# Delta rule by chunks of 64 tokens in place of 128, in a kernel of two layers

## The reference

```python
def step(S, inp):                                   # once a token
    q_t, k_t, v_t, b_t = inp
    pred = jnp.einsum('bhk,bhkv->bhv', k_t, S)
    delta = (v_t - pred) * b_t[..., None]
    S = S + k_t[..., :, None] * delta[..., None, :]
    o_t = jnp.einsum('bhk,bhkv->bhv', q_t, S)
```

## Time and profile before

| | us |
|---|---|
| median of 3 runs | 1889.7 |
| lowest of them | 1884.84 |
| the profiled execution: its time | 1893.3 |
| its span | 1891.7 |

### The profile page before, as it was taken

The page is one execution under the profiler, slowest core; times in us unless marked ns, Lnnn a source line. Parts: engine busy times, 40 slices in busy tenths (PEclk is TensorE's granted clock), DMA queues, the critical chain, the costliest instruction groups (busy, mean ns, idle before and its releaser), DMA issues. The chain is left out here.

```text
span 1891.7 us, 44267 instructions
## 1 busy us (share of the span) xinstructions
PE 1692.1 (89%) x16808; PEld 1123.2 (59%) x16808; DVE 1315.8 (70%) x3530; ACT 959.6 (51%) x2513; POOL 827.6 (44%) x827
## 2 busy tenths in 40 slices
PE   2698789998999999999999989999898999999787
PEld 1474557565775657656684657656575566755443
DVE  2654577767677778677777778687777778676373
ACT  1434544476345854467445754457534664456324
POOL 1725654554326444365436535265334554264000
PEclk9889989999799999999999999999989999999888
DMA  5220122201311023101222023200221013210020
GB/s 214 68 58 12 35 62 72 63 11 33 88 58 51 11 67 97 52 21 33 52 77 71 8 47 92 77 18 22 65 82 52 19 36 89 75 29 10 14 78 7
DMA packets 162147, 100.56 MB, mean 53 GB/s; under 512 B 59256, under 2 KB 149496, under 8 KB 161656
## 3 DMA queue, kind: packets, MB, share of 16 engines
q1 hardware_dynamic: 161648, 96.92, 19.2%
q10 hardware_dynamic: 288, 0.81, 0.2%
HBM read 55.36 MB, written 27.26 MB: 44 GB/s over the span
## 5 line engine op out<-in xcount | busy, mean ns | idle before, releaser
L1360 ACT ACTIVATE shared<-bank 128x512 f32<-128x512 f32 (+1 forms) x384 | 201.8, 532 | 205.9 <-PE bank L1067 203.6
L1834 POOL TENSOR_TENSOR soft<-soft,prec 128x512 f32<-128x512 f32 x128 | 132.5, 1041 | 371.8 <-DVE prec L1478 371.4
L1642 DVE TENSOR_REDUCE nmx<-bank 128x1 f32<-128x512 f32 (+3 forms) x352 | 222.9, 637 | 93.3 <-PE bank L1039 91.6
L1260 ACT ACTIVATE soft<-bank,nmax 128x128 f32<-128x128 f32 x512 | 180.2, 380 | 105.7 <-DVE nmax L1470 104.7
L1795 POOL TENSOR_TENSOR qk_rs<-qk_rs,minus_half 128x16 f32<-128x16 f32 x64 | 187.7, 2934 | 5.3
L718 PE MATMUL bank<-w_sb,hT 128*128 128x512 f32 x256 | 137.3, 627 | 5.6 <-DVE rot L1460 3.1
L1067 PE MATMUL bank<-shared 75*128 75x384 bf16 (+3 forms) x512 | 140.4, 302 | 0.0
L1066 PE MATMUL bank<-b_sb 128*128 128x128 bf16 x512 | 113.8, 224 | 25.6 <-ACT shared L1360 22.8
L1039 PE MATMUL bank<-shared 72*128 72x256 bf16 (+3 forms) x512 | 126.8, 300 | 0.0
L688 PE MATMUL bank<-c_sb,soft 128*128 128x128 f32 x608 | 98.6, 294 | 24.1 <-POOL soft L1834 18.1
L1066 PEld LDWEIGHTS bank<-b_sb 128*128 128x128 bf16 x512 | 48.9, 98 | 115.8 <-ACT shared L1360 70.3
(11 more groups left out here) (254 smaller groups left out, 4492.6 us busy)
## 6 DMA issues: line engine op xcount, KB each, us to landing
shared<-parts_dram SPq DMA_DIRECT2D x64, 288.0 KB
vm<-v_f SPq DMA_DIRECT2D x112, 128.0 KB, 2.4
parts_dram<-parts SPq DMA_DIRECT2D x96, 128.0 KB, 2.4
L_dram<-the SPq DMA_DIRECT2D x32, 256.0 KB, 2.3
shared<-Z_dram SPq DMA_DIRECT2D x32, 256.0 KB, 3.5
shared<-L_dram SPq DMA_DIRECT2D x32, 256.0 KB, 4.4
shared<-X_dram SPq DMA_DIRECT2D x32, 256.0 KB, 4.9
w_sb<-weights SPq DMA_DIRECT2D x1, 4167.0 KB, 19.7
```

What stands on the lines that cost most here:

```text
L1260: a = af(v4(p_sb, 2, 4)[:, j, g], place("fS", j)[:, g * P:(g + 1) * P], ACT.Exp, bias=nmax[:, at:at + 1], accum_out=psums[:, at:at + 1])
L1360: af(v4(PTm, 2, GROUP)[:, u % 2, i, 0:n], place("mST", b, i)[:, 0:n], ACT.Exp).then_inc(mexp_done, 1)
L1642: reduce(v3(nmx[:], HM)[:, h:h + len(heads), c], v3(place("mS", b, t)[:, 0:len(heads) * (c + 1) * P], len(heads)), AX, ALU.max, negate=Tru ...
L1834: tt(p, p, spread(prec[:, at:at + NPAIR], P), ALU.mult).then_inc(fnorm_done, 1)
```

## The change

A chunk of 128 tokens keeps its projections, its gram matrix and its mask step, but the sequence goes over halves of 64 tokens (`r` = 0, 1; s = 2c + r counts 8 of them). The inverse then ends at blocks of 64, so `LEVELS` is 3 and level 3 is gone; level 2 is now the last, and forms no X and no zero fill. `seq_p` no longer projects V: `vb` does it once a batch for all four chunks and DVE scales it by beta, so that R becomes two DVE operations; the first half of a sequence has S = 0, no `seq_p`, and takes `vb` as its R. `U_sb` holds two tiles, each with 64 rows that stay zero, so K' U and O still contract over 128 rows. K' U now goes ahead of O on PE. The last inverse product's own waits go, `inv_v` of chunk 0 waits for `vb` besides. All five tables of `ORDER` are new; of them the diff shows two lines.

```diff
-LEVELS = 4
+LEVELS = 3
+SUB = 64
+NS = T // SUB
...
-     "fefefededffefdddefeeeeffebefefbbbbfffbffbbfbfbfddddbfddfddbbddbddddbddbdddedbdbddbdbdbddddbdbbddbbddddbbdbddddff"
+     "fefefefefefdefeeeeffebeeffbbbbfffffbdbddddfbbfbbfddddbffddddbdbdbddbdbddddddddbdbddbdddbdbddddebdbbbbbddbdbddddfd"
...
-        R_sb, U_sb, Sn = sb("R_sb", P), sb("U_sb", P), sb("Sn", H0 * DV)
+        R_sb, U_sb, Sn = sb("R_sb", P), sb("U_sb", 2 * P), sb("Sn", H0 * DV)
...
+                def vb_(b):
+                    pe.wait_ge(qT_copied, H0 * (b + 1))
+                    for c in range(NT):
+                        m = mm(place("vb")[:, c * P:(c + 1) * P], xnT[:, c * P:(c + 1) * P], W("wv"), start=True, stop=True)
+                    m.then_inc(bg_psum, 1)
...
                     for h in range(H0):
-                        m = mm(place("B", c)[:, h * P:(h + 1) * P], kc[:, h], qT[:, h * T + c * P:h * T + (c + 1) * P], start=True, stop=True)
+                        for r in range(2):
+                            at = h * T + c * P + SUB * r
+                            m = mm(place("B", c)[rows(r), h * SUB:(h + 1) * SUB], kc[:, h, rows(r)], qT[:, at:at + SUB], start=True, stop=True,
+                                   skip_group_check=True)
...
+                def seq_p(b, c, r):
+                    s = 2 * c + r
+                    if c and r == 0:
+                        pe.wait_ge(o_copied, NT * b + c)
+                    pe.wait_ge(S_done, (NS - 1) * b + s)
+                    for h in range(H0):
+                        at = slice(h * DV, (h + 1) * DV)
+                        m = mm(place("P", c)[rows(r), at], v4(kT, NT, H0)[:, c, h, rows(r)], Sn[:, at], start=True, stop=True,
+                               skip_group_check=True)
+                    m.then_inc(P_psum, 1)
+
+                def seq_u(b, c, r):
+                    s = 2 * c + r
+                    if s:
+                        pe.wait_ge(R_done, (NS - 1) * b + s)
+                    right = R_sb if s else vb
+                    for h in range(H0):
+                        m = mm(place("U", c)[rows(r), h * DV:(h + 1) * DV], v4(Z, NT, H0)[rows(r), c, h, rows(r)],
+                               right[rows(r), h * DV:(h + 1) * DV], start=True, stop=True, skip_group_check=True)
+                    m.then_inc(U_psum, 1)
...
+                    tt(v3(vb, NT * H0), v3(place("vb")[:], NT * H0), spread(beta[:], DV), ALU.mult).then_inc(gs_done, 1)
...
+                    link(tt(v3(R_sb[rows(r)], H0), v3(place("P", c)[rows(r), 0:P], H0), spread(beta[rows(r), c * H0:(c + 1) * H0], DV), ALU.mult))
+                    tt(R_sb[rows(r)], R_sb[rows(r)], cols(vb, c, P)[rows(r)], ALU.add).then_inc(R_done, 1)
```

More of the change, by code:

```diff
@@ L47 @@
[L47 to L56, removed]
@@ L139, in constants @@
     i, j = np.arange(P)[:, None], np.arange(P)[None, :]
-    c = {"ident": np.eye(P, dtype=f), "strict": (j < i).astype(f), "upper": -(i <= j).astype(f)}
-    low = [-((i >> (k + 1) == j >> (k + 1)) & ((i >> k) & 1 == 1) & ((j >> k) & 1 == 0)).astype(f) for k in range(4, 7)]
+    c = {"ident": np.eye(P, dtype=f), "strict": (j < i).astype(f), "upper": -(i % SUB <= j[:, :SUB]).astype(f)}
+    low = [-((i >> (k + 1) == j >> (k + 1)) & ((i >> k) & 1 == 1) & ((j >> k) & 1 == 0)).astype(f) for k in range(4, 3 + LEVELS)]
     half = np.arange(0, DF, 2, dtype=f)
@@ L214, in steps_delta @@
 def steps_delta(b):
-    s = [("qT", b, h) for h in range(H0)] + [("bg", b)]
+    s = [("qT", b, h) for h in range(H0)] + [("bg", b), ("vb", b)]
     for two in ((0, 1), (2, 3)):
@@ L221, in steps_delta @@
         for c in two:
-            s += [("seq_b", b, c), ("seq_p", b, c), ("seq_u", b, c), ("seq_o", b, c)] + ([("seq_s", b, c)] if c < NT - 1 else [])
+            s += [("seq_b", b, c)]
+            for r in range(2):
+                s += ([("seq_p", b, c, r)] if c or r else []) + [("seq_u", b, c, r), ("seq_o", b, c, r)]
+                s += [("seq_s", b, c, r)] if 2 * c + r < NS - 1 else []
     return s + [("delta_back", b), ("delta_sum", b), ("delta_norm", b), ("oT0", b)]
@@ L607, in _ @@
             def _(pool):
-                for part in (warm[:], zeros, vm[:], hT[:, 0:1]):
+                for part in (warm[:], zeros, vm[:], hT[:, 0:1], U_sb[:]):
                     nc.gpsimd.memset(part, 0.0).then_inc(zeroed, 1)
@@ L1001, in seq_o @@
                         m.then_inc(dS_psum, 1)
-                def seq_s(b, c):
-                    pe.wait_ge(ST_done, (NT - 1) * b + c + 1)
+                    for k in range(2 if s else 1):
+                        for h in range(H0):
+                            left, at = (Sn[:] if k else u)[:, h * DV:(h + 1) * DV], h * T + c * P + SUB * r
+                            right = qT[:, at:at + SUB] if k else Bm[:, h * SUB:(h + 1) * SUB]
+                            m = mm(place("O", c)[h * DV:(h + 1) * DV, P + SUB * r:P + SUB * r + SUB], left, right, start=k == 0,
+                                   stop=k == (1 if s else 0), skip_group_check=True)
```

262 lines of the change are left out of this document (127 added, 135 removed).

## The result

| | us |
|---|---|
| changed kernel, median of 4 runs | 1915.7 (1912.02 to 1919.64) |
| kernel before, beside it | 1887.27 |
| ratio | 1.0162, 95% interval 1.0117 to 1.0207 |
| once more on another chip (below) | 1917.77 to 1883.67; 1.0200, 1.0161 to 1.0239 |

A forecast was written before the change was run, and what follows sets the result against it. PE, busy 1692 of 1892 us, was taken as the bound. From the profiled 1893.3 us, 23 of work and 4 of waits went and 28 of waits came: 1894.3, less 3.6 to the median, so 1891 us; range 1861 to 1920.

The forecast's parts named there:

- Work, step by step: PE's steps in each batch: 19.7 us go and 16.8 come, giving 23 us in all.
- inverse (level 3, X products): In each batch's inverse, level 3's steps go, 4.3 us, and level 2's X products, 1.9 us.
- the narrow steps' price of 0.59 us: Each `seq_p` and `seq_u` step on one 64-column tile costs PE 0.59 us, between ends of 0.33 and 0.91.
- rival (4): Narrow sequence steps cost PE what full-width ones do: 52 us more, 1943 us; chance 0.08.
- what stands behind U: Per batch after U: K' U 1.5 us, O 2.5 us with tiling changes, `seq_s` 0.8 us.
- +28 forecast in the sequence: PE waits added by 29 links a batch instead of 14: 28 us, bounds 0 and 56.
- -4 forecast for the inverse: PE's idle time of 3.7 us before level 3's first product goes: 4 us less.
- a link can land behind other work on DVE: Upper bound of added waits, 56 us: a link queued behind other work on DVE or ACT costs double.
- Rival (2): The added waits in the sequence are covered: 1863 us, or 1832 with cheap narrow steps too; chance 0.20.
- rival (3): The clock falls in more delta phases, 7.5 us each: 1929 us if all seven, three give 1914; chance 0.10.
- a sign that the forecast is wrong as a whole: Stretches between the delta phases, with new order tables, becoming longer or shorter by more than 2 us each.
- The other signs: PE busy falls 20 to 30 us; idle before `seq_u`, `seq_o` exceeds 20; seven later phases keep 65 to 70 us.

The follow-up runs named there:

- no_links: Changed kernel with the sequence's chain cut and every instruction kept, so it no longer computes the delta rule: 1875.65 us, ratio 0.9944.
- fill_links: Changed kernel with 81 unread full-width matmuls where chain steps stand next to each other on PE: 1900.63 us, ratio 1.0082.
- warm: Changed kernel with `gate_pick` cut into five steps and 226 unread matmuls wherever PE waits long or often: 1885.62 us, ratio 1.0031.
- before_warm: Kernel before, no step moved, with 185 unread full-width matmuls in front of PE's steps that wait: 1875.85 us, ratio 0.9931.

## Why the forecast was 25 us low

The number came out within the range and the mechanism for the most part: work given, waits of about that size added. The 25 us between are almost all a term that the sum did not have: work and idle time together, -15.6 and +19.6, add 4 us in the profiled execution, where the sum had +1, and 22 of its 26.3 us are left for the clock.

**Work, step by step.** Each step's median from its start to the next one's, idle time left out, times its number, gives for the touched steps 254.2 us before and 238.6 after: 15.6 given, where I had 23. (Summed as they ran, low clock included, they took 257.1 and 244.2 us.) Forecast and measured, in us:

| term | forecast | measured |
|---|---|---|
| inverse (level 3, X products) | -49.6 | -52.7 |
| `vb` | +7.2 | +7.9 |
| `seq_b` | -10.4 | -14.3 |
| `seq_p` | +6.6 | +3.6 |
| `seq_u` | +9.0 | +12.3 |
| `seq_o` | +10.4 | +15.7 |
| `seq_s` | +4.0 | +11.9 |

The inverse and the narrow steps' price of 0.59 us (0.58 for `seq_p`, 0.58 to 0.65 for `seq_u`) are right, and with that price rival (4), narrow steps as dear as full-width ones, is out. The term that was mis-sized is what stands behind U: K' U and O take 0.65 us together where I had 0.54, and `seq_s` 0.26 where I carried over 0.11. I had priced it from a place with full-width neighbours on both sides. Now a tiled step follows it in more than half of its 56 places, and it takes 0.26 to 0.33 there against 0.16 to 0.25 before a full-width one.

**Waits.** +28 forecast in the sequence, +34 measured in front of its steps (6 to 40 us); -4 forecast for the inverse, -6.5 measured (12.1 to 5.6). All of PE's idle time grew by 19.6, because the other streams waited 7 us less. The step was right, and so was the sentence that a link can land behind other work on DVE. (The links that it lists for batch 3 add to 4.8 us and not to 4.6, which changes nothing.) Rival (2), covered waits, is refuted: no_links shows them worth some 27 us.

**The clock.** This is the step that failed. The sum had no term for it, and rival (3) had 0.10. I had seen that a fall followed 7 us in which PE was busy 6.11, and counted phases in which it might happen. That count does not explain the time: rival (3) gave 1914 for three slow phases more than the two of before, and there is one more, three in place of two, which at its 7.5 us gives 1898. That 1915.7 lies near 1914 is luck. The falls are not tied to the inverse. Fillers in the links' gaps (fill_links) and in gaps all over the program (warm, before_warm) took them away, and 28 us of idle time in small pieces were being added by my own sum. Then the clock's part had to be the likeliest case and not a rival. Its size, known only afterwards, is 23 us by the rate, and 1891 + 23 is 1914; the comparison of warm with before_warm leaves less for it, about half of the loss. fill_links shows that the gaps in the links are a cause, and no coincidence; batch 3's fall stands behind another wait, that for the transfer, of which the prediction said that SP's transfers stay.

**The rest.** The stretches that follow the delta phases of batches 2 to 6, up to the next `qT`, are unchanged, 132.0 to 134.4 us against 131.5 to 134.6. The stretch from `qT` to the inverse grew from 87.3 to 101.6 us over batches 2 to 7, by `vb`, by steps of other streams that stand there now, and by 6 us of waits, 4 of them in batch 3. That is 14.3 of the 26.4 us by which the profiled span grew; the phases of batches 2 to 7 have 7.1. So a good half of the difference stands in front of the inverse, partly because work moved there out of the phases. From the end of one phase to the next inverse, three of the five stretches are 2.8 to 4.3 us longer, and `vb` accounts for about 1 of each. I had named a difference of over 2 us there as a sign that the forecast is wrong as a whole, and here it is. The new tables of order are thus a rival for part of the loss, and no run has the new chunks under another order.

**The other signs.** Idle time before `seq_u` and `seq_o` went from 6 to 21 us, as forecast. PE's busy time did not fall by 20 to 30 us but rose by 6.8, and of the seven phases only three kept 65 to 70 us.

## What to carry to other kernels

When a change trades work of the bounding engine for waits of the same size, the trade need not be even: here the waits of TensorE were paid a second time through its clock (0.0140 of it and 17 us came back when the 81 gaps were filled). So price a serial chain by its number of links, and every link by operation, hand-over, and the clock that its idle time costs; and where a link can't be covered, an unread matmul in the gap was cheap here. Look, too, at where a new order leaves the transfers: one of them, issued late, made a wait of 2.5 us in front of a fall of 13.7 us, which stood there in every version of the changed chain. Work that is taken from the bound was also cover for the chain beside it: of 51 us of inverse, 36 arrived.

## What the runs showed that I had not expected

- One program's runs differ by their clock: 1861.58 us at 0.988 and 1883.78 at 0.976 for before_warm, 1895.62 at 0.965 and 1911.09 at 0.957 for fill_links. A comparison of such kernels needs the clock of each run beside its time.
- In before_warm 40 fillers that took 9.09 us stand in a wait of 10.49 us, and left it at 10.64: matmuls that nobody reads cost next to nothing there, where they end before the operand comes.
- `seq_s`, one instruction, costs PE 0.11 us from start to start between full-width steps and 0.26 to 0.33 in front of a tiled one.
